# Third state scanned without its transpose, products in GpSimd's turns 6, 11 and 13, and the residual's layer norm made on ScalarE from a second load of x

## The reference

```python
x  = x + attn(layernorm(x))            # outer residual
# attn(y), with y = layernorm(x):
u  = layernorm(y, ln1)                 # the norm of a norm
xm, z = split(u @ in_proj.T)           # 512 + 512
xc = silu(conv4(xm) + conv_b)          # causal, 4 taps, per channel
dt, Bm, Cm = split(xc @ x_proj.T)      # 128 + 16 + 16
dt = softplus(dt @ dt_proj.T + dt_b)
for t in tokens:                       # 16 states per channel
    h = h * exp(dt*A) + dt * Bm * xc
    y_t = sum_s h * Cm
m  = (y_t + xc*D_skip) * silu(z) @ out_proj.T
x1 = y + m                             # inner residual: y is the FIRST layernorm
attn = x1 + gated_mlp(layernorm(x1, ln2))
# then a mixture of experts, 8 experts of rank 128, top 2, added to x
```

## Time and profile before

| what | value |
|---|---|
| three runs | 1285.03, 1285.68, 1286.23 us (median 1285.68) |
| the profiled execution | 1286.74 us, of it the span of the trace 1284.8 us |
| TensorE busy | 1197.1 us (93%) |
| ScalarE busy | 1089.1 us (85%) |
| GpSimd busy | 1019.4 us (79%) |
| VectorE busy | 995.6 us (77%) |

### The profile page before, as it was taken

One profiled execution on the slowest core, in us unless ns is written; L12 is line 12 of the kernel. 1 busy time (PEld: TensorE's weight loads), 2 busy tenths in 40 slices (PEclk: granted clock), 3 DMA queues, 4 the chain that ended last, 5 costly groups with the idle time before them and its releaser, 6 DMA issues.

```text
span 1284.8 us, 24309 instructions
## 1 busy us (share of the span) xinstructions
PE 1197.1 (93%) x7422; PEld 1029.2 (80%) x7422; DVE 995.6 (77%) x1800; ACT 1089.1 (85%) x2656; POOL 1019.4 (79%) x760
## 2 busy tenths in 40 slices
PE   5677989999999999999999999999999999998988
PEld 3466778888888888888888888888888888787876
DVE  2587987889797887879788887978889796887733
ACT  4888999899898989989898998989899998988621
POOL 2489798888888988888898888889888887888621
PEclk8797999999999999999999999999999999999999
DMA  2511102112221312222121222213121221203010
GB/s 69 199 58 52 65 19 105 46 52 90 67 92 34 100 43 64 79 68 91 42 94 43 69 72 69 92 36 98 43 75 67 68 83 53 87 36 99 17 50 17
DMA packets 33927, 86.83 MB, mean 68 GB/s; under 512 B 3592, under 2 KB 16512, under 8 KB 31360
## 3 DMA queue, kind: packets, MB, share of 16 engines
q1 hardware_dynamic: 33792, 85.20, 20.2%
HBM read 67.76 MB, written 4.84 MB: 57 GB/s over the span
## 4 chain that ended last, share of the span: by engine, by line
PE 67%; DVE 8%; issue 4%; ACT 2%; POOL 2%; DMA 2%; DVEq 0%; SPq 0%; ACTq 0%; POOLq 0%
PE psy L1359 11%; PE psx L1340 10%; PE pst L1220 8%; PE psb L1220 7%; PE psb L1214 6%; PE psf L1214 5%; PE pst L1214 4%; DVE h L1095 4%; PE psf L1308 2%; PE psf L1314 2%; PE psf L1258 2%; PE psf L1247 2%; PE psb L1314 2%; DVE acc L1059 2%; PE psb L1207 1%
## 5 line engine op out<-in xcount | busy, mean ns | idle before, releaser
L631 POOL TENSOR_TENSOR hC<-h,bC 128x1024 f32<-128x1024 f32 x256 | 604.5, 2368 | 126.1 <-DVE h L1095 116.8
L1095 DVE TENSOR_TENSOR_SCAN h<-dA,state,psx 128x256 f32<-128x256 f32 x896 | 597.2, 726 | 102.3 <-PE psx L1340 94.4
L871 ACT ACTIVATE dA<-dt,neg_a 128x256 f32<-128x256 f32 x896 | 380.1, 500 | 0.0
L1340 PE MATMUL psx<-ident,bxT 128*128 128x128 f32 x1792 | 270.5, 278 | 34.1 <-DVE h L1095 28.7
L1340 PEld LDWEIGHTS psx<-ident,bxT 128*128 128x128 f32 x1792 | 215.7, 143 | 74.4 <-issue 29.6
L1359 PE MATMUL psy<-ident,hC 128*128 128x128 f32 x2048 | 267.7, 274 | 3.9 <-POOL hC L631 3.9
L1359 PEld LDWEIGHTS psy<-ident,hC 128*128 128x128 f32 x2048 | 235.7, 142 | 10.6 <-POOL hC L631 4.7
L859 ACT ACTIVATE bxT<-uTs,BT 128x512 f32<-128x512 f32 x352 | 232.4, 715 | 5.9 <-PE psx L1340 3.1
L1220 PE MATMUL pst<-w_b_sb,cbc 128*128 128x256 f32 x480 | 110.8, 379 | 0.0
L1220 PEld LDWEIGHTS pst<-w_b_sb,cbc 128*128 128x128 f32 x480 | 90.1, 190 | 11.7
L882 ACT ACTIVATE psx<-dt,neg_a 128x256 f32<-128x256 f32 x128 | 55.3, 463 | 49.7 <-DVE h L1095 49.7
(11 more groups left out here) (178 smaller groups left out, 1894.5 us busy)
## 6 DMA issues: line engine op xcount, KB each, us to landing
bC<-bc_scratch SPq DMA_DIRECT2D x64, 512.0 KB, 4.0
cbc<-cw_scratch SPq DMA_DIRECT2D x15, 1024.0 KB, 4.7
uk<-sp_l SPq DMA_DIRECT2D x16, 512.0 KB, 6.3
xf<-in_x SPq DMA_DIRECT2D x16, 256.0 KB, 2.7
xk<-xn SPq DMA_DIRECT2D x16, 256.0 KB, 4.3
un<-bc_scratch SPq DMA_DIRECT2D x16, 256.0 KB, 4.1
xb<-in_x SPq DMA_DIRECT2D x16, 256.0 KB, 5.3
out<-x SPq DMA_DIRECT2D x16, 256.0 KB, 2.2
```

Of the source, the lines that this page charges most:

```text
L631: nc.gpsimd.tensor_tensor(hC[:, s % RC], h[:, ring(s)], bC[:, g % RINGG, s % G:s % G + 1, :].to_broadcast([P, NJ, T]), ALU.mult).then_inc( ...
L871: last = nc.scalar.activation(dA[:, s % RA, j, :], dt[:, n[1], j, :], ACT.Exp, scale=neg_a[:, j, s:s + 1])
L1095: last = nc.vector.tensor_tensor_scan(h[:, r, j, :], decays, inputs, state[:, b, j, s:s + 1], ALU.mult, ALU.add)
L1340: last = nc.tensor.transpose(psx[bx_bank(fill)][:, k, j * P:(j + 1) * P], bxT[:, s % RX, j, c:c + P], ident[:, :])
```

## The change

`DIRECT` becomes (13, 14, 15): no weighing, no transposes for state 13; ScalarE's exponentials of it go to PSUM in turn 12. GpSimd makes the product of 14 in turn 6, of 13 in turn 11, of 15 in turn 13; each has its own place, `bB` a tile of its own (three rows), loaded in turn 3 and no longer in 5. `xn`, `xk` and their copy are gone. ScalarE keeps the inverse deviation (`scales[..0]`) and minus the mean (`less`), GpSimd makes their product (`biases`, a 128x2 instruction), a tiny DMA keeps both, and ScalarE makes the norm in `back` 4 from `xb`, straight into `x1`; VectorE adds in place. `un` moves from GpSimd's turn 14 to 15, and `load_x` waits for `un` alone.

```diff
-DIRECT = (14, 15)
+DIRECT = (13, 14, 15)
-    return s - RX if s >= RX else (12, 13, 11)[s] - S
+    return s - RX if s >= RX else (12, 10, 11)[s] - S
...
             def load_x(m):
-                copied = value(count(1, m, 0))
-                sp.wait_ge(xn_done, copied)
-                if is_first(prev(m)):
-                    sp.wait_ge(un_done, 1)
+                gone = value(count(1, m, 0))
+                sp.wait_ge(un_done, gone)
...
                 if s == 8:
-                    sp.wait_ge(x1_done, gone)
-                    sp.wait_ge(xn_done, made)
-                    sp.dma_start(xk[:, m[1]], xn[:, m[1]]).then_inc(xk_copied, 16)
+                    sp.wait_ge(xn_done, gone)
+                    sp.wait_ge(biases_done, made)
+                    sp.dma_start(kept[:, m[1]], scales[:, m[1]]).then_inc(scales_kept, 16)
...
-                if part == 0 and s == 5:
-                    gone = value(count(len(IN_UNITS), n, 1 if is_late(n) else 2 * len(IN_UNITS) + 1))
-                    sp.wait_ge(filled_in, gone)
+                if part == 0 and s == 3:
+                    weighed = value(count(ND, n, 0))
+                    sp.wait_ge(direct_done, weighed)
                     sp.dma_start(bB[:, :, :], bc_scratch[n[1]][DIRECT[0]:DIRECT[0] + ND, :].partition_broadcast(P)
...
+            def biases(m):
+                b = m[1]
+                gone, made = value(count(16, m, -16)), value(count(1, m, 1))
+                pool.wait_ge(ident_ready, 1)
+                pool.wait_ge(scales_kept, gone)
+                pool.wait_ge(less_done, made)
+                pool.wait_ge(rstd_done[0], made)
+                nc.gpsimd.tensor_tensor(scales[:, b, 1, :], scales[:, b, 0, :], less[:, :], ALU.mult).then_inc(biases_done, 1)
...
-                if s == 14 and not is_last(m):
+                if s == 15 and not is_last(m):
+                    biases(following(m))
                     norm_again(following(m))
-                if s == 6:
...
-                        last = nc.gpsimd.tensor_scalar(xn[:, b, j, :], xf[:, j, :], mv[0][:, j, 0:1],
-                                                       rstd[0][:, j:j + 1], ALU.subtract, ALU.mult)
-                    last.then_inc(xn_done, 1)
...
-                if part == 0 and s in (11, 13):
-                    weigh_direct((11, 13).index(s), n)
+                if part == 0 and s in (6, 11, 13):
+                    weigh_direct({6: 14, 11: 13, 13: 15}[s], n)
...
             def first_deviations(m):
+                nc.scalar.activation(less[:, :], mv[0][:, :, 0], ACT.Copy, scale=-1.0).then_inc(less_done, 1)
...
             # ScalarE, back
+                if s == 4:
+                    act.wait_ge(xb_loaded, count(16, m, 16))
+                    act.wait_ge(scales_kept, count(16, m, 16))
+                    act.wait_ge(x1x_done, count(1, m, 0))
+                    for j in range(SUB):
+                        last = nc.scalar.activation(x1[:, j, :], xb[:, j, :], ACT.Identity, scale=kept[:, m[1], 0, j:j + 1],
+                                                    bias=kept[:, m[1], 1, j:j + 1])
+                    last.then_inc(xn_done, 1)
...
             # VectorE, back 6
-                    dve.wait_ge(xk_copied, count(16, m, 16))
-                    nc.vector.tensor_tensor(x1[:, :, :], xk[:, b], psb[:, :, :], ALU.add).then_inc(x1_done, 1)
+                    dve.wait_ge(xn_done, count(1, m, 1))
+                    nc.vector.tensor_tensor(x1[:, :, :], x1[:, :, :], psb[:, :, :], ALU.add).then_inc(x1_done, 1)
```

More of the change, by code:

```diff
@@ L235, in mamba_moe @@
         xf = sb("xf", [P, SUB, DM])
-        xn = sb("xn", [P, B, SUB, DM])
-        xk = sb("xk", [P, B, SUB, DM])
+        scales = sb("scales", [P, B, 2, SUB])
+        kept = sb("kept", [P, B, 2, SUB])
+        less = sb("less", [P, SUB])
         un = sb("un", [P, SUB, DM])
@@ L246, in mamba_moe @@
         lnv = [sb(f"lnv{k}", [P, SUB]) for k in range(4)]
-        rstd = [sb(f"rstd{k}", [P, SUB]) for k in range(4)]
+        rstd = {k: sb(f"rstd{k}", [P, SUB]) for k in (1, 2, 3)}
         minus = {k: sb(f"minus{k}", [P, SUB]) for k in (1, 2)}
@@ L306, in mamba_moe @@
         cT = nT[0:NE, 1, :]
-        bB = un
         def direct_inputs(s):
-            return (ygt[:, :, :].rearrange("p j (k t) -> p (j k) t", t=T), sp_e[:, :, :])[DIRECT.index(s)]
+            if s == 15:
+                return bx15[:, :, :]
+            return sp_e[:, :, :] if s == 13 else ygt[:, :, :].rearrange("p j (k t) -> p (j k) t", t=T)
+        direct_order = (14, 13, 15)
         def pairs(half):
@@ L546, in norm_again @@
                 last.then_inc(un_done, 1)
+            def biases(m):
[6 more added lines that the diff above has]
+                nc.gpsimd.tensor_tensor(scales[:, b, 1, :], scales[:, b, 0, :], less[:, :], ALU.mult).then_inc(biases_done, 1)
             def enter(s, m):
                 b = m[1]
-                if s == 14 and not is_last(m):
+                if s == 2 and is_first(m):
+                    biases(m)
+                if s == 15 and not is_last(m):
+                    biases(following(m))
                     norm_again(following(m))
-                if s == 6:
-                    copied, scaled = value(count(16, m, -16)), value(count(1, m, 1))
-                    pool.wait_ge(ident_ready, 1)
-                    pool.wait_ge(xk_copied, copied)
-                    pool.wait_ge(rstd_done[0], scaled)
-                    for j in range(SUB):
-                        last = nc.gpsimd.tensor_scalar(xn[:, b, j, :], xf[:, j, :], mv[0][:, j, 0:1],
-                                                       rstd[0][:, j:j + 1], ALU.subtract, ALU.mult)
-                    last.then_inc(xn_done, 1)
                 if s == 0:
@@ L611, in weigh_direct @@
                     pool.wait_ge(filled_back, count(len(BACK_UNITS), n, 2 - len(BACK_UNITS)))
-                else:
+                if s == 13:
                     pool.wait_ge(sp_rest, count(1, n, 1 if is_last(n) else 2))
-                nc.gpsimd.tensor_tensor(direct_inputs(DIRECT[i]), uk[:, :, :],
-                                        bB[:, i:i + 1, :].to_broadcast([P, NJ, T]), ALU.mult).then_inc(direct_done, 1)
+                if s == 15:
+                    pool.wait_ge(scan_done, count(FILLS, n, 0))
+                row = s - DIRECT[0]
+                nc.gpsimd.tensor_tensor(direct_inputs(s), uk[:, :, :], bB[:, row:row + 1, :].to_broadcast([P, NJ, T]),
+                                        ALU.mult).then_inc(direct_done, 1)
             def main(s, n, part):
-                if part == 0 and s in (11, 13):
-                    weigh_direct((11, 13).index(s), n)
+                if part == 0 and s in (6, 11, 13):
+                    weigh_direct({6: 14, 11: 13, 13: 15}[s], n)
                 if part == 0:
@@ L733, in first_deviations @@
                 act.wait_ge(lnv_done[0], count(1, m, 1))
-                nc.scalar.activation(rstd[0][:, :], lnv[0][:, :], ACT.Exp, scale=-0.5).then_inc(rstd_done[0], 1)
+                nc.scalar.activation(scales[:, b, 0, :], lnv[0][:, :], ACT.Exp, scale=-0.5).then_inc(rstd_done[0], 1)
                 act.wait_ge(lnv_done[1], count(1, m, 1))
```

16 lines of the change are left out of this document (10 added, 6 removed).

## The result

The changed kernel takes 1296.43 us (median of 10 runs, 1288.27 to 1307.91), the kernel before beside it 1285.36 us (10 runs, 1281.94 to 1290.09): ratio 1.0069, 95% interval 1.0044 to 1.0094. The ratio is one of means, without the longest execution (1307.91 us), which fell in the chip's slower state; the medians lie 11.1 us apart, the means 8.9. The kernel is slower by 0.7%, above the forecast's range of 1276 to 1290. The profiled execution of the changed kernel took 1299.1 us with a span of 1297.0, against 1286.74 and 1284.8 before; its mean granted clock is 0.973 against 0.979.

A forecast was written before the change was run, and what follows sets the result against it. The prediction took TensorE, in order and 93% busy, to bound steps 2 to 13. Its terms, -12.2 + 13.0 - 3.2 + 0.2 = -2.2 us, gave 1284.5 us against the profiled execution, 1283.5 us against the median; range 1276 to 1290.

The forecast's parts named there:

- State 13's transposes: Turn 12, steps 2 to 15: dropping state 13's fills saves TensorE 0.87 us a step, -12.2 us in all.
- freed time isn't used: Rival, turns 12 to 15: ScalarE's exponentials set the pace, the 12.2 us don't come, up to 1295.7 us; chance 0.07.
- The norm in turn 4: ScalarE's turn 4: two added activations delay taps and second projection by 1.00 us in 13 steps, +13.0 us.
- absorbed: Rival: turn 4's added work is not paid in full; half gives 1277 us, all 1270.5; chance 0.18.
- turn 4 dearer: Rival: the pair with its waits takes 1.3 us or inputs come late, 1287.4 to 1290.6 us; chance 0.11.
- The DMA order: Steps 14 and 15: `bB` issued in turn 3 lets the expert weights' store go and land sooner, -3.2 us.
- An edit counts by two questions: Steps 2 to 13, TensorE in order: an edit's worth is which TensorE instructions go and where TensorE now waits.
- the clock falls: Rival: TensorE's new wait in turn 5 lowers the granted clock every step, adding 44 us, 1328 us; chance 0.02.
- the 1 us wait of turn 5: Sign in turn 5: TensorE waits about 1.1 us for VectorE's taps in 13 steps.
- What costs nothing: GpSimd's product replaces the norm at the same place in turn 6; other moved work and loads also fit, at no cost.

The follow-up runs named there:

- run 11: The changed kernel with 17 tiny matmuls added, bringing the loop's start back to 176 of 256: 1282.27 us, ratio 0.9985.
- run 5: The kernel before with only the norm changed, made by ScalarE in turn 4; TensorE's program stays the same: 1295.65 us, ratio 1.0068.
- Run 2: The changed kernel with ScalarE's two norm activations moved from turn 4 to turn 5: 1285.11 us, ratio 0.9996.
- Run 1: The changed kernel with the load of the B rows (`bB`) put back from turn 3 to turn 5: 1295.55 us, ratio 1.0075.
- runs 3: The changed kernel with both the B rows' load and ScalarE's norm in turn 5: 1287.67 us, ratio 1.001.
- Run 12: Run 10 with GpSimd's product of state 14 in turn 10 in place of turn 6 in steps 14 and 15: 1269.53 us, ratio 0.9865.
- run 10: The changed kernel with ScalarE's norm in turn 5 and 17 tiny matmuls bringing the loop's start back to 176: 1270.42 us, ratio 0.9893.
- run 4: The kernel before with a further 384 KB load, which nobody reads, added in turn 3: 1286.89 us, ratio 1.0008.
- run 6: Run 2 with 34 tiny matmuls (136 instructions) ahead of everything, the loop starting at 244 of its piece: 1279.07 us, ratio 0.9962.
- 7: Run 2 with 64 tiny matmuls (256 instructions, a whole piece) ahead of the loop: 1295.34 us, ratio 1.0086.

## Why the prediction was wrong

The forecast's sum is near the change without the pauses: run 11 took 1282.27 us beside 1283.96, which is -1.7 us (by the interval of its ratio -3.7 to -0.1); the sum said -2.2. That it is so near is partly luck: the norm was priced 3 us too high and step 14's collision, some 3 us with the clock, wasn't in the sum. Term by term:

- **State 13's transposes, -12.2 us: right.** Changed kernel against run 5, which differ by the direct state with its products and by the DMA order, in steady steps: 73.95 against 74.83 outside the loop, -0.88 us, as forecast (0.87); in it 74.20 against 75.14, -0.94. Run 2 against the kernel before gives the same, 73.01 and 73.89. Steps 14 and 15 I can't separate. The gain is used up to the end of the step; the rival "freed time isn't used" is out.
- **The norm in turn 4, +13.0 us: right in kind, a little large.** 0.99 us from start to start, TensorE's wait 0.92 to 1.1 us in each step. Alone (run 5) it costs 10.0 us over 13 periods, since most of them grow by 0.7 and not by 1.0. Where these 0.3 us go I haven't traced. Moved by one turn (run 2) it costs nothing. The rivals "absorbed" and "turn 4 dearer" are both out.
- **The DMA order, -3.2 us: right for the waits, not shown for the time.** Run 1 gives 3.4 us of waiting for it. The times of steps 14 and 15 together differ by 1.6 us between run 1 and the changed kernel and not at all between runs 3 and 2, because the collision in step 14 changes with it.
- **"An edit counts by two questions: which of TensorE's instructions go, and where does TensorE now wait": this step failed.** There is a third, where TensorE's remaining instructions lie. Taking 68 of them out ahead of the loop moved its start from 176 to 108 of a piece of 256, and there TensorE pauses behind each of three jumps until the next packet of code is in. That is worth 13.0 us in the three periods of the profiled pair. In the total it is 11 to 14 us: 14.2 by the medians of the changed kernel and of run 11, which were timed apart, and 10.8 by their ratios to the kernel before beside each (1.0069 and 0.9985). It is more than the pauses themselves (2.6 + 3.7 + 2.7 = 9.0 us): behind the second and third the granted clock falls, which the rival "the clock falls" had tied to the 1 us wait of turn 5. In run 11 that wait stands in steps 1 to 13, and the window of steps 2 to 13 above has 1.00.
- **"What costs nothing": GpSimd's norm goes and a product comes "at the same place". Wrong in step 14.** The norm belongs to the entering chunk and has ended by then, the product belongs to the scanned one and goes on. There GpSimd has 2.36 us more to do, loses the 1.27 us it had idle, and runs its product beside VectorE's L1092. Run 12 prices it: the period of step 14 is 66.85 us without the collision, 68.4 to 68.6 with it, and 70.1 to 70.2 where the clock falls behind it too, so it cost 3.2 to 3.4 us in the changed kernel; against the kernel before, which lacks the two gains, it shows as +1.8. I counted 16 steps as one kind where the last two have another set of stages.

None of my rivals held the pauses, and no row that I had read shows them: in the trace of before, the loop happens to start where they don't arise. What could have warned me is there: the packets of code behind each jump, 6 us apart. In the changed kernel the idle time of L1365's weight loads put down to "issue" is 41.2 us, 29.6 for the same line before.

One thing stays open. The runs show which of four places within a piece is bad, not why that one; the trace doesn't tell which instruction a packet holds, nor for which engine it is, so that TensorE waits for this very packet is inferred from the 18 jumps at which it goes on right behind it. The length of a pause (2.2 to 3.9 us) follows from when the packet ends.

## What to carry to other kernels

Before crediting the removal of instructions from an engine that runs a long loop, look for pauses put down to "issue" a few microseconds behind each jump back, in the kernel before and after, and try the change with its code shifted: here 68 idle instructions were worth 11 to 14 us, about as much as the largest term of the change. Compare period by period, not only the total: the loss stood in 4 of 15 periods. And read a wait's worth in the period of its step, not in the wait: shorter DMA waits in step 14 met a longer collision behind them. And check an edit that swaps one piece of work for another in every kind of step, the opening and the last ones too, where one of the two may be missing. The best versions here are the change with the norm one turn later and the loop's start where it was (run 10, 1270.42 us) and the same with state 14's product later in the last two steps (run 12, 1269.53), by their ratios 1.1 and 1.4% faster than the kernel before.

## What the hardware showed that I had not expected

- Packets of 16 KB of code arrive behind each jump of the loop. With the loop's start at 108 of 256 TensorE pauses for 2.2 to 3.9 us at its 85th instruction behind a jump, in six kernels with different code, and goes on 1.2 to 1.6 us after the second packet has ended; at 40, 176 and 244 it doesn't pause. All kernels, before included, also have a shorter pause of 0.7 to 1.5 us at the 32nd.
- A transfer of 384 KB at the same time isn't what makes the pause: without it the pause stays (run 1), and added to the kernel before it makes none (run 4).
- A wait of TensorE of 2.0 to 2.3 us in step 14 was followed by a lower granted clock in three kernels (2.29, 2.07 and 2.30 us; changed, 10, 11) and not in three others (2.32, 1.96 and 2.01 us; 2, 6, 7). Where it fell, the step took 1.5 to 1.8 us more.
- One fp32 matmul of 8 columns shows as two weight loads and two matmuls, and 136 such instructions at the very start make the start 10.5 us longer (run 6), 188 ahead of the loop 10 us, 376 25 us, while the 68 of run 10 cost nothing that the start shows.
- VectorE and GpSimd can block each other by turns: VectorE's 1.75 us became 2.60, 3.22 or 4.29, or its 0.68 us became 2.86 with GpSimd's 2.36 at 3.35 beside it. Which one it is changes with where GpSimd stands.
